# Other orders of the same work on every engine of a two-batch attention and LoRA kernel

## The chip, the cores and the metric

One Trainium2 chip, one core of it. The metric is the device time of one launch in microseconds, the median of several runs. PE is the engine of matrix products and of transposes, PEld its weight loads, DVE the vector engine, ACT the scalar engine, POOL GpSimd, SP the engine that issues most DMAs.

## What is computed

For each of two batches of 1024 tokens (512 features): a layer norm, attention with 32 query heads in 8 groups of 4 (one key and value head per group, rms-normed queries and keys, a causal mask with a slope per head), the output projection, the residual; then a second layer norm and a mixture of 8 LoRA adapters, with its residual.

```python
q = _rmsnorm(q, q_norm_w); k = _rmsnorm(k, k_norm_w)
scores = jnp.einsum('bkgqd,bksd->bkgqs', qg, k) / math.sqrt(HD)
attn = jax.nn.softmax(scores + bias[None], axis=-1)
out = jnp.einsum('bkgqs,bksd->bkgqd', attn, v)
...
x = x + _L0_attn_ref(_layernorm(x, axis=-1), ...)      # out @ Wo.T inside
low = jnp.einsum('bsd,hrd->bshr', x, A)
out = jnp.einsum('bshr,hor,bsh->bso', low, B, scores)
x = x + _L0_ffn_ref(_layernorm(x, axis=-1), ...)
```

## The kernel before

The work is cut into 16 **groups** w = 0 to 15: eight head groups of the first batch, then the same eight of the second. A group holds 8 tiles s of 128 queries, and 4 heads h. The names of the items, as the tables have them:

- `q.8.c` to `q.15.c` and `q.1.c` to `q.7.c`: the projection of one query tile in four parts; `square_q` (ACT), `inv_q` (POOL), `norm_q` (DVE) norm it, `turn.q` transposes it on PE, `high.q` (ACT) and `low.q` (DVE) split it in an upper and a lower fp32r part. A number of 8 or more is a tile of the next group: each group prepares tiles 0 and 1 of its successor, and its keys and values (`turn.kv`, `inv_k`, `norm_k`, `turn.k`, `v_high`, `v_low`).
- `scores.s.h` (PE) into one PSUM tensor of two banks, `max.s.h` (DVE: bias, row maximum, copy to SBUF), `exp.s.h` (ACT), `invert.s.i` (DVE), `normalise.s.h` (POOL).
- The weights of a query tile have to be transposed in tiles j. Some go over PE: `turn.p.s.j`, `high.p`, `low.p`. The others go **through memory**: `send_p.s.h` (SP) stores a head's row to HBM, `fetch_p.s.j` (SP, four DMAs each) loads a tile back in transposed order of blocks, `flip_p.s.j` (DVE) transposes within blocks, `upper_p.s.j` (ACT) and `lower_p.s.j` (POOL) split. The first `fetch_p` of a tile waits until all four sends of it have landed.
- `values.s.j` (PE) accumulates over j, the tiles through memory last, `o_high.s` (ACT) and `o_low.s` (DVE) split the result, `y.s` is the output projection, `add_y.s` (DVE) the residual.
- `x_stats`, `x_moments`, `x_rstd`, `x_norm`, `turn.x`: the first layer norm; `f_...`, `turn.f`, `turn.logits`, `turn.lora`, `f_out`, `add_f`: the second one and the LoRA mixture, one tile at a time.

Every product is done in three matmuls (upper by upper, lower by upper, upper by lower; line 1106). Every transpose on PE goes through one of three PSUM banks in turn.

**What sets the order.** No scheduler runs at build time. Six tables of items stand at the top of the file (lines 27 to 299): `PROLOGUE` (before group 0), `GROUP_A` (groups 0 to 6), `BOUNDARY` (group 7, which also starts the second batch and the first batch's LoRA part), `FIRST_B` (group 8), `GROUP_B` (groups 9 to 14), `LAST` (group 15). `follow` (line 423) goes through them once per engine and emits those items that belong to that engine, so each table is the order of all five engines at once, and each engine executes its items strictly in that order. An item waits for semaphores alone: an item that waits holds up everything behind it on its engine. The semaphores count, so the wait values follow from the positions in the tables.

Tiles through memory and their buffers are set apart from the order: `MEMORY_TILES` says which tiles j of each query tile take that way. In groups 0 to 6 there are two more pairs of split buffers than in group 7; in groups 8 to 15 two more pairs and two more raw buffers (`MORE_SLOTS, MORE_RAW = (2, 0, 2), (0, 0, 2)`).

## Time and profile before

| | us |
|---|---|
| median of 3 runs | 2059.68 |
| lowest, highest | 2056.29, 2061.45 |
| the profiled execution | 2058.6 |
| its span, first to last instruction | 2056.5 |

In that execution PE is busy for 97% of the span, PEld 83%, DVE 66%, POOL 58%, ACT 57%, and the TensorE clock was granted in full for 99.7% of it. In the rows further down a time is microseconds from the start of the span; "[0.74 <-DVE oT_lo L1029]" behind a row is idle time of that engine ahead of it, and what ended it. A PE row's duration overlaps with its successor's, so the distance between two starts says what a matmul takes of the engine, and the idle time in brackets is shorter than the time lost by what the overlap adds.

### The profile page before, as it was taken

To read this page: it belongs to the slowest core of one execution; us is meant where nothing else is said; L and a number is where in the kernel's file an instruction comes from. 1 tells how busy PE (TensorE), PEld (TensorE's weight loads), DVE (VectorE), ACT (ScalarE), POOL (GpSimd) and SP (SyncE) were. 2 spreads that over 40 slices of the span, in tenths; PEclk is the share of its full clock that TensorE was granted. 3 is DMA by queue.
4 is the path that set the end of the run, shared out by engine and by line. 5 is a ranking of instruction groups with operands and counts; after the bars stand their busy time and mean duration, and the time that the engine had idled before them with its cause. 6 is when DMAs were issued, how large, how long until landed. Compare 5 with 4: busy or idle time off the path is not lost.

```text
span 2056.5 us, 33589 instructions
## 1 busy us (share of the span) xinstructions
PE 1993.2 (97%) x10956; PEld 1698.1 (83%) x10956; DVE 1363.5 (66%) x3431; ACT 1162.6 (57%) x3314; POOL 1189.2 (58%) x1188
## 2 busy tenths in 40 slices
PE   7999999999999999999999899999999999999996
PEld 6888888888888888888888788787878878788774
DVE  6667667666666666768876566565666656566696
ACT  4656656565665656655555465555656555465552
POOL 3574645647465574655645557465664746657473
PEclk9999999999999999999999999999999999999998
DMA  4573855657466573765635637365463745637254
GB/s 164 138 161 119 192 141 150 132 154 166 129 171 145 136 159 113 181 181 142 135 109 141 142 96 173 96 154 139 123 124 108 172 101 137 161 81 165 69 122 99
DMA packets 896141, 283.81 MB, mean 138 GB/s; under 512 B 677721, under 2 KB 839513, under 8 KB 895969
## 3 DMA queue, kind: packets, MB, share of 16 engines
q1 hardware_dynamic: 844064, 179.44, 41.7%
q10 hardware_dynamic: 51904, 102.24, 14.2%
q8 instruction: 88, 1.44, 0.3%
q14 instruction: 85, 0.69, 0.1%
HBM read 152.59 MB, written 128.97 MB: 137 GB/s over the span
## 4 chain that ended last, share of the span: by engine, by line
PE 76%; SPq 8%; DMA 4%; DVE 4%; issue 4%; POOL 2%; ACT 2%; DVEq 0%; POOLq 0%; ACTq 0%
PE s_ps L1106 16%; PE q_ps L1106 15%; PE y_ps L1106 14%; PE o_ps L1106 14%; PE turn_ps L1193 9%; SPq L653 7%; PE turn_ps L1106 7%; DMA p_bounce<-probs_odd 2%; POOL probs_odd L881 1%; DMA p_raw_b<-p_bounce 1%; DMA p_bounce<-probs_even 1%; DVE oT_lo L1029 1%; PE turn_ps L1187 1%; SPq L642 1%; ACT oT_hi L823 1%
## 5 line engine op out<-in xcount | busy, mean ns | idle before, releaser
L881 POOL TENSOR_TENSOR probs_odd<-probs_odd,p_inv 128x256 f32<-128x256 f32 (+3 forms) x256 | 318.0, 1257 | 180.1 <-DVE p_inv L1008 179.2
L881 POOL TENSOR_TENSOR probs_even<-probs_even,p_inv 128x128 f32<-128x128 f32 (+3 forms) x256 | 261.3, 1043 | 191.3 <-DVE p_inv L1008 190.5
L1106 PE MATMUL s_ps<-kT_hi,qT_hi 128*128 128x512 f32 (+3 forms) x768 | 272.5, 355 | 4.1 <-DVE neg_max L1001 3.8
L1001 DVE CUSTOM_DVE_ANT_0 probs_odd<-s_ps,rel 128x256 f32<-128x256 f32 (+3 forms) x256 | 209.3, 820 | 97.3 <-issue 96.6
L802 ACT ACTIVATE probs_odd<-probs_odd,neg_max 128x256 f32<-128x256 f32 (+3 forms) x256 | 212.2, 831 | 91.7 <-DVE neg_max L1001 91.6
L1106 PE MATMUL s_ps<-kT_hi,qT_lo 128*128 128x512 f32 (+3 forms) x768 | 262.4, 342 | 0.0
L1106 PE MATMUL s_ps<-kT_lo,qT_hi 128*128 128x512 f32 (+3 forms) x768 | 261.7, 341 | 0.0
L802 ACT ACTIVATE probs_even<-probs_even,neg_max 128x128 f32<-128x128 f32 (+3 forms) x256 | 185.1, 725 | 118.7 <-DVE neg_max L1001 118.4
L1001 DVE CUSTOM_DVE_ANT_0 probs_even<-s_ps,rel 128x128 f32<-128x128 f32 (+3 forms) x256 | 174.9, 687 | 109.8 <-issue 108.8
L987 DVE STREAM_TRANSPOSE p_raw<-p_raw 128x512 f32<-128x512 f32 x252 | 174.9, 700 | 83.5 <-DMA p_raw<-p_bounce 83.2
L1106 PE MATMUL q_ps<-wqT_hi,xnT_hi 128*128 128x512 f32 x512 | 217.2, 424 | 1.0 <-DVE qn L1012 0.8
L1106 PE MATMUL y_ps<-woT_hi,oT_hi 128*128 128x512 f32 x512 | 204.8, 400 | 10.9 <-DVE oT_lo L1029 8.6
L789 ACT ACTIVATE pT_hi<-turn_ps 128x512 fp32r<-128x512 f32 x260 | 154.3, 597 | 107.3 <-PE turn_ps L1193 107.3
L887 POOL TENSOR_TENSOR pT_lo<-p_raw,pT_hi 128x512 fp32r<-128x512 f32 x134 | 173.8, 1301 | 49.7 <-ACT pT_hi L797 49.6
L1106 PE MATMUL q_ps<-wqT_hi,xnT_lo 128*128 128x512 f32 x512 | 201.6, 394 | 0.0
L1106 PE MATMUL y_ps<-woT_hi,oT_lo 128*128 128x512 f32 x512 | 200.5, 392 | 0.0
L1106 PE MATMUL q_ps<-wqT_lo,xnT_hi 128*128 128x512 f32 x512 | 200.4, 391 | 0.0
L1106 PE MATMUL y_ps<-woT_lo,oT_hi 128*128 128x512 f32 x512 | 199.9, 390 | 0.0
L979 DVE TENSOR_TENSOR pT_lo<-turn_ps,pT_hi 128x512 fp32r<-128x512 f32 x260 | 174.8, 677 | 27.2 <-ACT pT_hi L789 26.1
L811 ACT ACTIVATE qn<-q_ps 128x128 f32<-128x128 f32 x512 | 134.7, 280 | 94.9 <-PE q_ps L1106 93.9
L1106 PE MATMUL o_ps<-pT_hi,v_hi 128*128 128x512 f32 x426 | 177.3, 416 | 4.5 <-DVE pT_lo L979 3.7
L1106 PEld LDWEIGHTS s_ps<-kT_hi,qT_hi 128*128 128x128 f32 x768 | 144.6, 188 | 32.0 <-DVE neg_max L1001 9.1
(131 smaller groups left out, 5068.3 us busy)
## 6 DMA issues: line engine op xcount, KB each, us to landing
p_raw<-p_bounce SPq DMA_DIRECT2D x1008, 64.0 KB, 2.3
p_bounce<-probs_odd SPq DMA_DIRECT2D x60, 384.0 KB, 3.1
p_raw_b<-p_bounce SPq DMA_DIRECT2D x256, 64.0 KB, 2.4
p_bounce<-probs_odd SPq DMA_DIRECT2D x60, 256.0 KB, 2.8
p_bounce<-probs_even SPq DMA_DIRECT2D x60, 256.0 KB, 3.0
p_bounce<-probs_even SPq DMA_DIRECT2D x64, 192.0 KB, 2.4
wq_kept<-wqT_hi ACTq DMA_DIRECT2D x8, 1024.0 KB, 4.5
wq_kept<-wqT_lo ACTq DMA_DIRECT2D x8, 1024.0 KB, 6.8
```

Source lines behind the costliest of these rows:

```text
L642: sp.dma_start(p_bounce[s % 2, first:s + 1, h].rearrange("u p c -> p u c"), probs[s % 2][:, h, first * P:(s + 1) * P].rearrange("p (u c) - ...
L653: sp.dma_start(raw_p(n)[b * BLOCK:(b + 1) * BLOCK, :].rearrange("p (n j) -> p n j", j=BLOCK), blocks[b]).then_inc(p_fetched[n], 16)
L789: nc.scalar.activation(target, bank, ACT.Copy).then_inc(sems["high"], 1)
L802: nc.scalar.activation(row, row, ACT.Exp, bias=neg_max[:, s % 2, h:h + 1], scale=-1.0, accum_out=p_sum[:, s % 2, h:h + 1]).then_inc(sems[" ...
L811: last = nc.scalar.activation(qn[:, h, :], q_ps[:, h * HD:(h + 1) * HD], ACT.Square, scale=float(slopes[gg % NG * G + h]), accum_out=q_sum ...
L881: nc.gpsimd.tensor_tensor(row, row, p_inv[:, s % 2, h:h + 1].to_broadcast((P, L)), ALU.mult).then_inc(sems["normalise"], 1)
L887: nc.gpsimd.tensor_tensor(p_low(r), raw_p(raw_tile[w, s, j]), p_high(r).bitcast(F32), ALU.subtract).then_inc(sems["lower_p"], 1)
L979: nc.vector.tensor_tensor(target, bank, upper.bitcast(F32), ALU.subtract).then_inc(sems["low"], 1)
L987: nc.vector.transpose(raw, raw).then_inc(sems["flip_p"], 1)
L1001: nc.vector.tensor_tensor_reduce(out=probs[s % 2][:, h, 0:L], in0=s_ps[:, at_col:at_col + L], in1=rel[:, S - L:S], scale=-float(slopes[w % ...
L1106: last = nc.tensor.matmul(target, a, m, start=start and i == 0 and k == 0, stop=stop and i == len(pairs) - 1 and k == 2)
L1193: last = nc.tensor.transpose(bank[0:width, i * rows:(i + 1) * rows], source, ident[0:rows, 0:rows])
```

## The change

The six tables of items are written in another order. Each table holds exactly the items that it held before (125, 502, 666, 507, 469 and 573), and everything behind them is unchanged but for one line of shift (line 1106 is 1107 afterwards): the same instructions, `MEMORY_TILES`, buffers and rule of waits. No item moves from one table to another. The lines below are the heads of two tables; the rest of the diff is of this kind.

```diff
 PROLOGUE = (
-    "load_y.2 load_y.0 load_y.1 load_y.3 load_y.7 x_stats.2 load_y.4 x_stats.0 load_y.6 x_stats.1 load_wkv.first "
+    "load_y.1 load_y.0 load_y.2 load_y.3 load_wkv.first x_stats.1 x_moments.1 x_stats.0 x_rstd.1 load_wq.first "
...
 GROUP_B = (
-    "back_wkv scores.0.0 scores.0.1 norm_q.1 max.0.0 max.0.1 turn.q.1 exp.0.0 q.2.0 back_wo scores.0.2 high.q.1 q.2.1 "
+    "back_wkv scores.0.0 scores.0.1 norm_q.1 max.0.0 max.0.1 turn.q.1 exp.0.0 q.2.0 high.q.1 q.2.1 exp.0.1 back_wo "
```

**PE, first third of group 0 (table `GROUP_A`), query tile 1.** `s_ps` 128x256 are the scores of tile 1, three matmuls for each head; `w_raw` is a weight being transposed. Before:

```order
L1193 MATMUL turn_ps<-ident,w_raw 128x128 x4
L1106 MATMUL s_ps<-kT_hi,qT_hi 128x256
L1106 MATMUL s_ps<-kT_lo,qT_hi 128x256
L1106 MATMUL s_ps<-kT_hi,qT_lo 128x256
L1106 MATMUL s_ps<-kT_hi,qT_hi 128x256
L1106 MATMUL s_ps<-kT_lo,qT_hi 128x256
L1106 MATMUL s_ps<-kT_hi,qT_lo 128x256
L1106 MATMUL s_ps<-kT_hi,qT_hi 128x256
L1106 MATMUL s_ps<-kT_lo,qT_hi 128x256
L1106 MATMUL s_ps<-kT_hi,qT_lo 128x256
L1193 MATMUL turn_ps<-ident,w_raw 128x128 x4
```

And in the same place now:

```order
L1194 MATMUL turn_ps<-ident,w_raw 128x128 x4
L1107 MATMUL s_ps<-kT_hi,qT_hi 128x256
L1107 MATMUL s_ps<-kT_lo,qT_hi 128x256
L1107 MATMUL s_ps<-kT_hi,qT_lo 128x256
L1107 MATMUL s_ps<-kT_hi,qT_hi 128x256
L1107 MATMUL s_ps<-kT_lo,qT_hi 128x256
L1107 MATMUL s_ps<-kT_hi,qT_lo 128x256
L1194 MATMUL turn_ps<-ident,w_raw 128x128 x4
L1107 MATMUL s_ps<-kT_hi,qT_hi 128x256
L1107 MATMUL s_ps<-kT_lo,qT_hi 128x256
L1107 MATMUL s_ps<-kT_hi,qT_lo 128x256
L1194 MATMUL turn_ps<-ident,w_raw 128x128 x4
```

`turn.wkv.0`, which stood behind head 2, now stands between heads 1 and 2 of tile 1, and `turn.wo.3` (the last row) now stands between heads 2 and 3.

**SP, second half of a group of batch B (table `GROUP_B`).** `p_bounce<-probs_even 128x4x128` are the sends of tile 6, `p_bounce<-probs_odd 128x6x128` those of tile 7 (heads 0 to 3 in order), `x4` of `p_raw` or `p_raw_b` is one `fetch_p`. Before:

```order
L642 DMA p_bounce<-probs_even 128x4x128 x4
L653 DMA p_raw<-p_bounce 32x16x32 x8
L642 DMA p_bounce<-probs_odd 128x6x128
L653 DMA p_raw<-p_bounce 32x16x32 x4
L642 DMA p_bounce<-probs_odd 128x6x128
L653 DMA p_raw_b<-p_bounce 32x16x32 x4
L642 DMA p_bounce<-probs_odd 128x6x128 x2
L653 DMA p_raw_b<-p_bounce 32x16x32 x4
```

And now:

```order
L643 DMA p_bounce<-probs_even 128x4x128 x3
L654 DMA p_raw<-p_bounce 32x16x32 x12
L643 DMA p_bounce<-probs_odd 128x6x128
L654 DMA p_raw_b<-p_bounce 32x16x32 x4
L643 DMA p_bounce<-probs_odd 128x6x128 x3
L654 DMA p_raw_b<-p_bounce 32x16x32 x4
```

`fetch_p.6.5` now stands ahead of `send_p.7.0`, and `fetch_p.6.6` ahead of `send_p.7.1`, so nothing stands between the last three sends of tile 7.

**DVE, group 8 (table `FIRST_B`), from the copy `kv_raw` of the last keys on.** `STREAM_TRANSPOSE` is a `flip_p`, `pT_lo<-turn_ps,pT_hi` a `low.p`. Before:

```order
L952 COPY kv_raw<-turn_ps 128x512
L987 STREAM_TRANSPOSE p_raw<-p_raw 128x512
L979 TENSOR_TENSOR pT_lo<-turn_ps,pT_hi 128x512
L1029 TENSOR_TENSOR oT_lo<-o_ps,oT_hi 128x512
L979 TENSOR_TENSOR pT_lo<-turn_ps,pT_hi 128x512
L987 STREAM_TRANSPOSE p_raw<-p_raw 128x512
L987 STREAM_TRANSPOSE p_raw_b<-p_raw_b 128x512
L1035 TENSOR_TENSOR y<-y_ps,y 128x512
L979 TENSOR_TENSOR pT_lo<-turn_ps,pT_hi 128x512
L1018 TENSOR_TENSOR kv_raw<-kv_raw,k_inv 128x8x128
```

And now:

```order
L953 COPY kv_raw<-turn_ps 128x512 x2
L988 STREAM_TRANSPOSE p_raw<-p_raw 128x512
L1036 TENSOR_TENSOR y<-y_ps,y 128x512
L1030 TENSOR_TENSOR oT_lo<-o_ps,oT_hi 128x512
L980 TENSOR_TENSOR pT_lo<-turn_ps,pT_hi 128x512 x2
L988 STREAM_TRANSPOSE p_raw<-p_raw 128x512
L1019 TENSOR_TENSOR kv_raw<-kv_raw,k_inv 128x8x128
L980 TENSOR_TENSOR pT_lo<-turn_ps,pT_hi 128x512
L988 STREAM_TRANSPOSE p_raw_b<-p_raw_b 128x512 x2
```

The `flip_p.6.6` on `p_raw_b` stood ahead of `add_y.4` and of the last `low.p` of tile 6 (`low.p.6.2`); now it stands behind both.

## Rows read from the trace of the kernel before

**Rows 1.** Busy time by stretch: groups 3, 7, 8, 10 and 15.
```profile
core 0: us, PE busy (x) PEld busy (x) DVE busy (x) ACT busy (x) POOL busy (x), PEclk, DMA share, GB/s
408.70:532.40 123.70, 122.85 (x685) 105.78 (x685) 81.92 (x199) 74.34 (x210) 72.78 (x70) 1.00 0.60 149
903.40:1046.60 143.20, 142.05 (x810) 120.03 (x811) 119.92 (x320) 77.10 (x218) 78.50 (x92) 1.00 0.56 150
1046.60:1176.80 130.20, 124.29 (x675) 105.34 (x675) 83.86 (x218) 69.17 (x205) 74.16 (x74) 1.00 0.57 140
1299.10:1420.50 121.40, 118.69 (x645) 101.41 (x644) 75.45 (x188) 68.89 (x200) 72.97 (x70) 1.00 0.55 131
1908.50:2056.50 148.00, 129.34 (x645) 101.25 (x643) 110.53 (x293) 66.61 (x188) 76.05 (x82) 0.96 0.43 100
```

**Rows 2.** Timeline of PE, group 4: start, duration, engine, line, operation, tiles.
```profile
542.43 0.39 PE L1106 MATMUL s_ps<-kT_hi,qT_hi 128*128 128x256 f32 x1 [0.31 <-DVE neg_max L1001]
542.65 0.28 PE L1106 MATMUL s_ps<-kT_lo,qT_hi 128*128 128x256 f32 x1
542.77 0.28 PE L1106 MATMUL s_ps<-kT_hi,qT_lo 128*128 128x256 f32 x1
...
549.07 0.39 PE L1106 MATMUL q_ps<-wqT_lo,xnT_hi 128*128 128x512 f32 x1
549.30 0.40 PE L1106 MATMUL q_ps<-wqT_hi,xnT_lo 128*128 128x512 f32 x1
```

**Rows 3.** Timeline of PE: `y.7` of group 3, `turn.q.1` of group 10.
```profile
532.37 0.50 PE L1106 MATMUL y_ps<-woT_hi,oT_hi 128*128 128x512 f32 x1 [0.54 <-DVE oT_lo L1029]
...
1303.55 0.63 PE L1193 MATMUL turn_ps<-ident,qn 128*128 128x128 f32 x4 [0.92 <-DVE qn L1012]
```

**Rows 4.** Timeline of PE, end of group 10: `y.6`, `values.7.6`, `values.7.7`.
```profile
1407.84 0.50 PE L1106 MATMUL y_ps<-woT_hi,oT_hi 128*128 128x512 f32 x1 [0.74 <-DVE oT_lo L1029]
...
1416.31 0.50 PE L1106 MATMUL o_ps<-pT_hi_b,v_hi 128*128 128x512 f32 x1 [0.87 <-POOL pT_lo_b L887]
...
1417.88 0.51 PE L1106 MATMUL o_ps<-pT_hi_b,v_hi 128*128 128x512 f32 x1 [0.18 <-POOL pT_lo_b L887]
```

**Rows 5.** Timeline of SP and POOL, group 10, after `scores.7.3` (ended 1388.8).
```profile
1392.90 3.57 SPq L653 DMA_DIRECT2D p_raw_b<-p_bounce  x4
1396.51 1.08 SPq L642 DMA_DIRECT2D p_bounce<-probs_odd  x2
1400.79 1.93 SPq L653 DMA_DIRECT2D p_raw_b<-p_bounce  x4
1409.21 4.15 SPq L653 DMA_DIRECT2D p_raw_b<-p_bounce  x8
...
1391.76 3.75 POOL L881 TENSOR_TENSOR probs_odd<-probs_odd,p_inv 128x1024 f32<-128x1024 f32 x2 [0.61 <-DVE p_inv L1008]
```

**Rows 6.** Timeline of DVE and PE, group 8: `flip_p.6.6`, `low.p.6.2`, `values.6.2`.
```profile
1154.04 0.71 DVE L987 STREAM_TRANSPOSE p_raw_b<-p_raw_b 128x512 f32<-128x512 f32 x1 [3.43 <-DMA p_raw_b<-p_bounce]
...
1155.25 0.67 DVE L979 TENSOR_TENSOR pT_lo<-turn_ps,pT_hi 128x512 fp32r<-128x512 f32 x1
...
1155.98 0.50 PE L1106 MATMUL o_ps<-pT_hi,v_hi 128*128 128x512 f32 x1 [3.03 <-DVE pT_lo L979]
```

**Rows 7.** Timeline of SP, group 8: `fetch_p.6.6` and the last two sends.
```profile
1149.30 2.51 SPq L653 DMA_DIRECT2D p_raw_b<-p_bounce  x4
1151.86 1.08 SPq L642 DMA_DIRECT2D p_bounce<-probs_odd  x2
```

**Rows 8.** Timeline of POOL, group 15: `lower_p.6.3`, the last two norms of tile 7.
```profile
2006.18 1.28 POOL L887 TENSOR_TENSOR pT_lo_b<-p_raw,pT_hi_b 128x512 fp32r<-128x512 f32 x1
2007.64 3.75 POOL L881 TENSOR_TENSOR probs_odd<-probs_odd,p_inv 128x1024 f32<-128x1024 f32 x2 [0.19 <-DVE p_inv L1008]
```

**Rows 9.** Timeline of DVE and PE, the start: first row tile, `q.8.2`.
```profile
3.45 1.33 DVE L907 BATCH_NORM_STATS2 x_stat<-y 128x6 f32<-128x512 f32 x2 [1.63 <-DMA y<-in_L_attn_x]
...
22.54 0.48 PE L1106 MATMUL q_ps<-wqT_hi,xnT_hi 128*128 128x512 f32 x1
```

517 rows, old and new, of tables (BOUNDARY, FIRST_B, GROUP_A, GROUP_B) are left out of this document.

## Prediction

> **What bounds the kernel.** I read the busy times by stretch first [rows 1]. PE is busy for 122.85 of 123.70 us of group 3, 142.05 of 143.20 in group 7, 124.29 of 130.20 in group 8, 118.69 of 121.40 in group 10 and 129.34 of 148.00 in group 15; the next engine is DVE, with at most 119.92 of 143.20. So PE is the bound nearly everywhere, its clock is granted in full, and what an order can win is the time in which PE stands still. How much that is cannot be read from busy time, because successive matmuls overlap in the records. The starts tell it [rows 2]: 0.23 us from one 512-column matmul to the next although each lasts 0.40, and 0.12 for 256 columns. A row's bracket therefore understates a stop: the last matmul's overhang (0.40 - 0.23) and the longer first one behind it (0.50 instead of 0.39 or so) belong to it too. `y.7` of group 3, with 0.54 in its bracket [rows 3], loses about 0.9 against a string without a stop.
>
> Added up over the timeline of PE in this way, the stops are: 10.1 us before the first PE instruction; about 1.5 in each of groups 0 to 6 (2 to 3 in the first two); 3.9 in group 7; 7.9 in group 8; 3.5 to 5 in each of groups 9 to 14; 22.7 in group 15, of which 13 lie in the chain behind the last attention output, whose items stand as before. All of it together is some 83 us, and no more than that can go. PE's own work is the same in either order, so it gives nothing back by itself. What follows goes through the stops and asks of each: how long is the chain that it waits for, how much PE work stands between that chain's start and the waiting item (the **cover**, the sum of the starts' distances of what stands between), and what the new order does to both.
>
> **Batch A, groups 0 to 6.** Two stops have a plain change. `scores.1.2` waits for the row maximum of `scores.1.0` (0.31 in the bracket [rows 2], about 0.6 lost): the chain takes 0.77, the cover was 0.36, one triple of 0.12s. The new order puts `turn.wkv.0`, four transposes, between: cover 0.72, so 0.05 to 0.1 is left and 0.5 won. `y.7` waits for `o_low.7`, a chain of 1.5 behind `values.7.7` with a cover of 0.7 in both orders [rows 3]: stays. The others (0.3, 0.15, 0.15) move here and there. I take -0.6 a group, seven times: -4, bounds 0 and -5 (a new stop as large as the old; and half of what is there gone).
>
> **Group 7.** Its 3.9 us are spread over DVE waits of 0.2 to 0.9; about half of them get a longer cover, while several covers of the tiles through memory shrink by 1 to 4 us, which their slack bears as far as the trace tells. -1.5, bounds 0 and -3.
>
> **Batch B, groups 9 to 14**, is the largest term. Here the stops stand at the end [rows 4]: `y.6` (0.74 in the bracket), `values.7.6` (0.87, for POOL's `lower_p.7.6`) and `values.7.7` (0.18), about 2.7 with the overlap, and they come from one chain. `scores.7.3` ends at 1388.8. POOL norms heads 2 and 3 of tile 7 from 1391.76 to 1395.51, so the last head could be sent from 1395.5 at the latest. It isn't: SP is inside `fetch_p.6.6`, four issues that take 3.57 us from 1392.90, and the two last sends go out from 1396.51 to 1397.59 [rows 5]. They land, `fetch_p.7.2` starts at 1400.79, and six fetches of about 2.1 us each follow until 1413.36; then flip, upper and lower part of the last tile: 29.1 us from `scores.7.3` to the ready `lower_p.7.7`, for a cover of 25.9. In the new order `fetch_p.6.5` and `fetch_p.6.6` stand ahead of the sends of tile 7 and were issued by the time at which POOL ends. The last send then starts with POOL's end, 1.0 to 1.4 earlier (1396.51 - 1395.5, and the wait for the first of the two falls away), and everything behind it moves by the same, since SP runs through from there. The cover is 26.2. So the end stops lose up to 1.4 + 0.3, which is all of their 1.7, and `y.6` is the next in turn. It waits for `o_low.6`; that item now stands behind `flip_p.7.3` on DVE, whose data land some 1.4 earlier too, so I expect it ready at about the time at which PE gets there, and its 1.0 to stay between 0.3 and 1.3. `turn.q.1` (0.92 in the bracket [rows 3]) has the same neighbours and stays. I keep the 0.3 back for it: -1.4 a group, six times: **-8.4**. Bounds: 0 (the fetches are limited by landing and not by SP's place) and -12 (both stops gone, 2.0 a group).
>
> **Group 8.** The same tail: `fetch_p.6.6` takes SP from 1149.30 to 1151.81 and the last two sends follow at 1151.86 [rows 7], while POOL had normed the last head by 1148.85; behind the move, 1.3 earlier. The largest single stop is another: `flip_p.6.6` waits 3.43 for its landing at the head of DVE's queue, and the `low.p.6.2` behind it, which needs no data from memory, holds `values.6.2` (3.03 in the bracket) [rows 6]. The new order puts the flip behind both `low.p`. But PE doesn't win these 3.4: the chain from `scores.7.3` to the last tiles takes 32.2 for a cover of 27.5 in both orders, so most of what is saved early is waited for at `values.7.x`. What is won in the end is what the chain itself becomes shorter, 1.3, the stop at `scores.0.2` (0.8, its cover grows from 0.34 to 2.06) and about 0.9 of small ones: -3, bounds -1 and -6 (the whole 3.4 stays won).
>
> **Group 15.** POOL does `lower_p.6.3` (1.28) ahead of the norms of tile 7, which run from 2007.64 to 2011.39 [rows 8]. The new order norms first, and `exp.7.3` isn't behind the upper part of tile 6 any longer: 2.0 less from `scores.7.3` to the last send. `scores.7.3` itself stands 1.3 of PE work later, and some 2.2 of stops ahead of it get cover. -2.0 + 1.3 - 2.2 = **-2.9**, bounds +2 (the later scores count in full and the rest stays) and -6.
>
> **The start.** PE starts at 10.1 on `turn.x`. The first row tile lands at 3.4 [rows 9] and one follows each 0.6 to 1.8 behind it. The new order loads tile 1 first and norms it first, which makes its `turn.x.1` ready about 3.5 earlier. That is no gain by itself: DVE has 16.5 us of work between 3.4 and 23.2, and `q.8.2` at 22.54 [rows 9] needs the end of it in either order. 0, bounds -1 and +1.5.
>
> **Waits not seen before.** With 2,842 items in other places some covers shrink whose wait the trace doesn't show: in group 7 as above, at `values.7.4` of group 8, at `values.3.0` in batch A. Each has a margin in the trace of before, but the margins are 1 us and less for the worst of them. I take +2, bounds 0 and +8 (0.5 a group, what the small stops of batch A cost now).
>
> **Sum.** -4 - 1.5 - 8.4 - 3 - 2.9 + 0 + 2 = -17.8. The profiled execution took 2058.6, so 2040.8; the median of the runs is 1.1 above it, so **2042**. The bounds of the terms taken together in opposite directions are not likely at once; half of them either way gives about 2033 to 2052.
>
> **Rivals.**
>
> *Nearly every stop goes* (0.12). A search over whole tables may have found cover for `turn.q.1`, `y.6` and `y.7` that I don't credit. For it: DVE has 38% of its time free in group 10 [rows 1]. Against it: `turn.q.1` and `y.7` have the same neighbours. 4 us for batch A, 3 for group 7, 3 x 6 for groups 9 to 14 (their 3.5 to 5 without `turn.q.1`), 4 and 3 for groups 8 and 15, +2 for new waits: -30 in place of -17.8, so 2030 after the same 1.1.
>
> *The order isn't what holds the ends of batch B* (0.14). The stops at `values.7.6` and `values.7.7` recur in each of its groups at the same place, and the fetches into `p_raw_b` come one by one: if `fetch_p.7.2` may not start before the sends have landed and each later one before its raw buffer is free, an earlier send shifts only the first. Against it stands that SP shows its issues without a gap from 1400.79 on [rows 5]. Terms of batch B and group 8's tail are then 0: -4 - 1.5 - 1.7 + 2 = -5, 2054, no change that a measurement tells.
> The Trainium skill ("Perfetto Trace Analysis", Identifying Performance Opportunities) says that the same gap repeating on the engine that should be saturated can mean too little SBUF or PSUM for the next tile. By that rule, nothing is won here without more buffers, and the time is the one just given; the rows of SP speak for its order instead.
>
> *POOL is late for tile 7* (0.06), the case on the other side. In the new order of batch B the four `lower_p.5.2` to `5.5`, 1.28 each [rows 8], stand ahead of the norms of tile 7, where two stood behind the first of them. If `invert.7.0` is ready before POOL has done them, the norms run up to 2 x 1.3 = 2.6 later, the send of the last head too, and 2.6 - 1.4 - 0.3 = +0.9 a group replaces -1.4. It decides where POOL reaches `normalise.7.0` later than `invert.7.0` by over 1.7; in the trace of before POOL still waited 0.61 for the last `invert` [rows 5], which speaks against it. With +5.4 for groups 9 to 14, the same in 7, 8 and 15 (+7.5 instead of -7.4), +2 at the start and the gain of batch A eaten: about +14, 2073.
>
> **Chances.** The forecast has 0.68. 0.3%, 6 us, is about what a measurement of this kernel can tell from no change, so faster means below 2053.5. Faster has the forecast and the first rival, 0.80; same has the second, 0.14; slower the third, 0.06. The range reaches to 2031, near the large gain, and to 2056, which takes in the case of no change and leaves out the slow one.
>
> **What would show it.** In the profile after: the last two sends of tile 7 in groups 9 to 14 right behind POOL's second norm, with no `fetch_p` of tile 6 between, and `fetch_p.7.2` about 11 us after the end of `scores.7.3` instead of 12; the stop at `values.7.6` under 0.3, the one at `y.6` still there; groups 9 to 14 at 120 us instead of 121.4. `scores.1.2` of batch A without a bracket. Group 8: no 3 us bracket at `values.6.2`, but larger ones at `values.7.x`. `q.8.2` within 1 us of 22.5. It would be wrong if SP waits ahead of `fetch_p.7.2` for landings that don't move with the send, if DVE waits at a flip with a `low.p` or `o_low` behind it, or if POOL's norms of tile 7 start later than 3 us after `scores.7.3`.

## Result and profile after

The changed kernel takes 2065.83 us (median of 15 runs, 2062.13 to 2074.69), the kernel before 2058.18 in the same comparison: ratio 1.0045, with a 95% interval of 1.0034 to 1.0055. Forecast were 2042 and a faster kernel; it is slower by 0.45%, 9 us (7.7 between the two medians). Its profiled execution has a span of 2065.3 us against 2056.5.

Busy time by stretch of the changed kernel, the same columns as in [rows 1], groups 3, 7, 8, 10 and 15. Here a stretch goes from the start of one group's first scores to that of the next; the stretches of [rows 1] begin 2.8 to 3.7 us ahead of the first scores, so lengths are compared in the table further down, where both kernels are cut alike:

```profile
core 0: us, PE busy (x) PEld busy (x) DVE busy (x) ACT busy (x) POOL busy (x), PEclk, DMA share, GB/s
414.22:538.79 124.57, 122.83 (x688) 105.99 (x686) 82.09 (x199) 74.24 (x210) 73.91 (x70) 1.00 0.60 148
912.69:1055.50 142.81, 141.44 (x811) 119.77 (x809) 122.11 (x319) 77.70 (x224) 80.03 (x94) 1.00 0.53 140
1055.50:1182.12 126.62, 124.33 (x675) 105.05 (x675) 82.53 (x216) 69.41 (x203) 74.81 (x74) 1.00 0.59 147
1304.50:1425.40 120.90, 118.67 (x645) 101.37 (x644) 75.37 (x188) 69.02 (x199) 73.67 (x71) 1.00 0.55 131
1916.24:2065.30 149.06, 127.49 (x633) 101.40 (x631) 109.16 (x291) 65.15 (x179) 74.86 (x81) 0.94 0.43 99
```

PE's busy time in groups 3, 7, 8 and 10 is what it was, to 0.7 us; what differs is the stops. Group by group, from the starts of the first scores in the two profiles (the differences are taken before rounding):

| stretch | before | after | difference | forecast |
|---|---|---|---|---|
| start | 41.2 | 38.1 | -3.1 | 0 |
| groups 0 to 6 | 865.8 | 874.6 | +8.7 | -4 |
| group 7 | 142.4 | 142.8 | +0.4 | -1.5 |
| group 8 | 130.2 | 126.6 | -3.6 | -3 |
| groups 9 to 14 | 731.6 | 734.1 | +2.5 | -8.4 |
| group 15, to the end of `add_f.7` | 142.7 | 146.5 | +3.8 | -2.9 |

The last column leaves out the +2 for waits not seen before. Group 7's first two weight transposes stand behind its first scores now, which moves 0.7 us from the row of groups 0 to 6 to that of group 7.

**Groups 0 to 6.** All seven have one new stop, ahead of `scores.7.2`, of 0.96 to 2.09 us in its bracket. Timeline of DVE, PE, SP and ACT's DMA queue in group 4 of the changed kernel:

```profile
611.23 1.22 DVE L1002 CUSTOM_DVE_ANT_0 probs_odd<-s_ps,rel 128x1024 f32<-128x1024 f32 x1
612.38 1.30 DVE L988 STREAM_TRANSPOSE p_raw<-p_raw 128x512 f32<-128x512 f32 x2
617.00 0.71 DVE L988 STREAM_TRANSPOSE p_raw<-p_raw 128x512 f32<-128x512 f32 x1 [3.32 <-DMA p_raw<-p_bounce]
617.64 1.22 DVE L1002 CUSTOM_DVE_ANT_0 probs_odd<-s_ps,rel 128x1024 f32<-128x1024 f32 x1
...
618.92 0.50 PE L1107 MATMUL s_ps<-kT_hi,qT_hi 128*128 128x512 f32 x1 [1.60 <-DVE neg_max L1002]
...
605.43 6.77 SPq L654 DMA_DIRECT2D p_raw<-p_bounce  x12
612.29 4.55 SPq L643 DMA_DIRECT2D p_bounce<-probs_even  x4
...
609.70 0.43 ACTq L711 DMA_DIRECT2D w_raw<-in_L_attn_Wo  x1
```

The two `CUSTOM_DVE` rows are `max.7.0` and `max.7.1`, the three transposes `flip_p.5.2` to `5.4`. PE had finished `scores.7.1` at 614.45, but `max.7.1` starts at 617.64, because `flip_p.5.4` stands ahead of it and waits 3.32 us for its data; `scores.7.2` needs the PSUM that `max.7.1` reads. The issue of the fetch's last DMA ended at 612.20 and it landed close to 617.0, 4.8 us later. At 609.70, together with the first of the fetch's four DMAs, ACT issued `load_wo`, 1 MB.

**Groups 9 to 14.** The SP order is what was forecast, and it doesn't bring the gain. Timeline of SP in group 10, after `scores.7.3` (ended 1391.2); POOL's last norms; PE's `values.7.6` and `values.7.7` (compare [rows 4, 5]):

```profile
1393.05 0.43 SPq L643 DMA_DIRECT2D p_bounce<-probs_odd  x1
1393.59 2.47 SPq L654 DMA_DIRECT2D p_raw_b<-p_bounce  x4
1396.10 3.00 SPq L643 DMA_DIRECT2D p_bounce<-probs_odd  x3
1402.74 1.91 SPq L654 DMA_DIRECT2D p_raw_b<-p_bounce  x4
...
1394.03 3.75 POOL L882 TENSOR_TENSOR probs_odd<-probs_odd,p_inv 128x1024 f32<-128x1024 f32 x2 [0.86 <-DVE p_inv L1009]
...
1418.00 0.51 PE L1107 MATMUL o_ps<-pT_hi_b,v_hi 128*128 128x512 f32 x1
...
1420.02 0.51 PE L1107 MATMUL o_ps<-pT_hi_b,v_hi 128*128 128x512 f32 x1 [1.05 <-POOL pT_lo_b L888]
```

Three sends go out in one string from 1396.10 to 1399.10, no `fetch_p` between them, and `fetch_p.7.2` starts at 1402.74: 11.5 us after `scores.7.3` instead of 11.9. The stops at `y.6` and, mostly, at `values.7.6` are gone in all six groups; the one at `values.7.7` has grown (brackets of 1.05 to 2.15, where they were 0.18 to 0.83).

**The clock.** The granted clock is half for a short while behind a stop of PE, in group 2 of the changed kernel, and again in groups 11 and 12 and twice in group 15 ahead of the kernel's end. Busy time in stretches of 2 us, in group 2:

```profile
366.00:368.00 2.00, 0.23 (x1) 0.24 (x2) 1.71 (x4) 0.88 (x2) 0.71 (x1) 1.00 1.07 265
368.00:370.00 2.00, 2.00 (x8) 1.58 (x8) 0.60 (x3) 0.99 (x2) 1.30 (x2) 0.79 0.70 113
370.00:372.00 2.00, 2.00 (x6) 1.52 (x6) 2.00 (x4) 1.17 (x2) 2.00 (x2) 0.50 0.72 113
372.00:374.00 2.00, 2.00 (x9) 1.66 (x8) 0.02 (x1) 1.20 (x6) 2.00 (x2) 0.85 0.77 123
```

In the first 2 us PE worked for 0.23; then the granted clock is 0.79, 0.50 (1.2 of 2.4 GHz) and 0.85 of full speed, and the matmuls of `y.4` lie 1.6 us further apart in sum. Of the seven it is the only group in which this happened; it takes 126.90 where the others take 124.3 to 125.0. The length of the stop alone doesn't tell it: group 2's has 1.92 in its bracket, group 6's 2.09, and there the clock stayed full. One stretch of group 6 and one of group 11, each just behind the stop:

```profile
868.00:870.00 2.00, 1.35 (x6) 1.13 (x7) 0.69 (x3) 1.34 (x3) 1.29 (x1) 1.00 0.99 188
1544.00:1546.00 2.00, 2.00 (x7) 1.51 (x7) 0.69 (x1) 1.55 (x2) 0.00 (x0) 0.50 0.00 0
```

In groups 11 and 12 the half clock comes behind `values.7.7`, and from its start to the next group's first scores PE takes 6.96 us instead of the 5.38 of the groups beside them. These two times 1.6 us are more than the whole +2.5 in the row of groups 9 to 14.

### The profile page after: what moved, and what is told of

Read it like the earlier page. It is cut to its first block, busy times and chain, and to the rows that moved or that the text cites. A ratio compares the mean times of both kernels' runs of the same rounds, so it can differ in the third digit from the quotient of the medians.

```text
span 2065.3 us, 33588 instructions
## 1 busy us (share of the span) xinstructions
PE 1997.0 (97%) x10956; PEld 1704.7 (83%) x10956; DVE 1369.8 (66%) x3431; ACT 1162.0 (56%) x3314; POOL 1197.7 (58%) x1188
## 4 chain that ended last, share of the span: by engine, by line
PE 67%; DMA 8%; DVE 7%; issue 6%; SPq 6%; POOL 3%; ACT 2%; ACTq 0%; POOLq 0%; DVEq 0%
PE q_ps L1107 14%; PE s_ps L1107 13%; PE y_ps L1107 13%; PE o_ps L1107 12%; PE turn_ps L1194 8%; PE turn_ps L1107 6%; SPq L654 6%; DMA p_bounce<-probs_odd 4%; DMA p_raw<-p_bounce 3%; POOL probs_odd L882 2%; DVE p_raw L988 1%; DVE pT_lo L980 1%; DMA p_raw_b<-p_bounce 1%; DVE oT_lo L1030 1%; ACT probs_odd L803 1%
## 5 line engine op out<-in xcount | busy, mean ns | idle before, releaser
L1107 PE MATMUL s_ps<-kT_hi,qT_hi 128*128 128x512 f32 (+3 forms) x768 | 271.3, 353 | 13.3 <-DVE neg_max L1002 11.9
```

Source lines behind the costliest of these rows:

```text
L1107: last = nc.tensor.matmul(target, a, m, start=start and i == 0 and k == 0, stop=stop and i == len(pairs) - 1 and k == 2)
```

## Experiments

A group of lines under an edit is the order of the table, reduced to the items that matter. The ratios are to the kernel before, five rounds each, with their 95% intervals.

### One table at a time

```diff
-GROUP_A = (table of the kernel before)
+GROUP_A = (table of the changed kernel)
```

> The kernel before with the new GROUP_A alone (groups 0 to 6). In the profile of the changed kernel PE stops 1.3 to 2.2 us ahead of scores.7.2 in each of these groups, where it didn't before. Theory Q (the queue of DVE): flip_p.5.4 now stands ahead of max.7.1, its data land 3.3 us after DVE gets to it, and scores.7.2 waits for max.7.1. The loss belongs to this table alone: groups 0 to 6 together 8 to 10 us longer than before, scores.7.2 with a stop of 1.3 to 2.2 in each, time 0.4 to 0.5% above before (about 2067). Theory C (the clock): the granted clock of the whole execution fell from 0.997 to 0.993, which is 8 us of 2060; then this kernel without the new last group shows a clock of 0.996 or 0.997 and at most 2 us. Theory N (the neighbours): the stop comes from where the new table of the start leaves the DMA queues; then it is not there.

1.0037 (1.0024 to 1.0051), 2064.83 us. Groups 0 to 6 take 872.2 us, 6.3 more than before; `scores.7.2` has its stop in each (brackets of 0.81 to 2.18). Theory Q holds, though 6.3 is less than the 8 to 10 expected, and N falls: the stop needs nothing from the other tables. C isn't what carries it: in this profile the clock is full from the first to the last of these groups, and the loss is there.

```diff
-GROUP_B = (table of the kernel before)
+GROUP_B = (table of the changed kernel)
```

> The kernel before with the new GROUP_B alone (groups 9 to 14). In the two profiles the last send of tile 7 starts 6.9 us after the end of scores.7.3 instead of 7.8 (means of six groups), but fetch_p.7.2 only 11.8 instead of 12.0, and lower_p.7.7 ends 29.7 instead of 29.5 behind it. Theory D (the send lands no earlier): groups 9 to 14 are between 1 us shorter and 4 us longer in sum, the time within 0.2% of before. Theory V (chance): the 0.9 us of the earlier send are real and this one profile hid them; then the six groups are 5 us shorter, fetch_p.7.2 at 11.2 or less in the mean, -0.25%.

1.0002 (0.9993 to 1.0011). The send is early again (6.9), `fetch_p.7.2` at 11.8, groups 9 to 14 take 729.3. In the eight profiles taken in this study with the old table these six groups took 726.8 to 733.5, 729.4 in the mean; in the four with the new one 729.3 to 734.1, 732.0. So single profiles differ by more than the two tables do, and the +2.5 of the first comparison is no loss that can be told from none; this profile, the one of the four without a half clock in these groups, has 729.3. The gain forecast, 8.4, is not there: theory D. The same twelve profiles say it of the chain: with the old table the last send starts 7.5 us after `scores.7.3` in the mean and `fetch_p.7.2` at 11.6, with the new one 7.0 and 11.8. The 12.02 of the kernel before's own profile is at the high end.

```diff
-LAST = (table of the kernel before)
+LAST = (table of the changed kernel)
```

> The kernel before with the new LAST alone (group 15). Two places of DVE's queue in the profile of the changed kernel: max.7.3 starts 3.1 us after the end of scores.7.3, behind f_norm.4, low.p.6.1, f_low.3 and low.lora.2; and add_y.6 stands behind flip_p.7.4, whose data land 2 us after y.6 is ready, which turn.f.6 waits for (a stop of 3.4 on PE). Theory Q: group 15 takes 3.5 to 4.5 us longer than before wherever it stands, with the same two waits; +0.2%. Theory C: it is the half clock of 2 to 3 short stretches between 2010 and 2045; where the clock stays at 1.00 there, the group takes at most 1.5 us longer.

1.0022 (1.0012 to 1.0031). Group 15 takes 149.1; with the new table it took 146.5 to 149.1 in four profiles, with the old one 142.5 to 143.9 in eight. `max.7.3` starts 3.10 after `scores.7.3` and `turn.f.6` stops again (3.14 in its bracket). The loss belongs to the table. How much of it is clock (theory C) isn't separated: in this profile the clock is half for 6.8 us of the group, ahead of the half clock at the kernel's end that every profile shows, and in the kernel before for none.

```diff
-PROLOGUE, FIRST_B = (tables of the kernel before)
+PROLOGUE, FIRST_B = (tables of the changed kernel)
```

> The kernel before with the new PROLOGUE and the new FIRST_B (group 8). In the profile of the changed kernel the first scores stand at 38.1 us instead of 41.2 and group 8 takes 126.6 instead of 130.2. Theory S (both gains are real and add up): 6.7 us less, 0.9967 of before, first scores at 38.1 to 38.6, group 8 at 126.6 to 127.5. Theory G (given back later): what comes earlier at the start is waited for again in group 0, or group 9 is longer by what group 8 saved; then at most 2 us of them stay, 0.999.

0.9962 (0.9950 to 0.9975), 2048.07 us. First scores at 38.04, group 8 126.3, group 0 as before: nothing is given back. Theory S.

The four parts, timed apart, make +7.6, +0.4, +4.5 and -7.8 us, +4.7 in sum, against +9.2 for all of it; each is known to 2 or 3 us, so this sum agrees with the whole without proving it. `BOUNDARY` (group 7) wasn't timed by itself.

### Groups 0 to 6: the flip, the load, or both

The changed kernel with tile 5.4 put back:

```diff
 flip_p.5.3 scores.7.1 upper_p.5.2 exp.7.0
-flip_p.5.4
 ...
 turn.kv.0 max.7.1 upper_p.5.3
-upper_p.5.4
 ...
 exp.7.1
-lower_p.5.4 invert.7.0
+upper_p.5.4 invert.7.0 flip_p.5.4
 ... normalise.7.0
+lower_p.5.4
```

> The changed kernel with one tile through memory put back in GROUP_A: flip_p.5.4 behind invert.7.0 (DVE), upper_p.5.4 behind exp.7.1 (ACT), lower_p.5.4 behind normalise.7.0 (POOL), as in the kernel before. Theory Q: max.7.1 runs when scores.7.1 is there, the stop ahead of scores.7.2 is gone in groups 0 to 6 (under 0.2) and nothing takes its place (values.5.4 comes 8 us later), so the groups take 123.3 each instead of 124.9: 9 to 11 us less than the changed kernel, 2055 to 2057, that is -0.1% against before. Theory L (late landing as such): what is late is fetch_p.5.4; the stop moves to values.5.4 or y.5 and at most 3 us are won. Theory C: at most 2 us.

0.9982 (0.9972 to 0.9991), 2052.45 us, below the 2055 to 2057 expected: the three items were worth 0.63% against the changed kernel, and turned it from slower to faster. The stop at `scores.7.2` is gone and none takes its place; groups 0 to 6 take 861.7, 12.9 less than in the changed kernel, of which the seven stops make some 11.4 and the half clock of group 2 1.6. Theory Q, as far as the place of the flip is one way to remove the loss. The landing isn't earlier by it: the fetch's last DMA still lands 4.6 to 6.5 us behind the end of its issue, only nothing urgent waits for it. Then the flip's new place alone, in the kernel before:

```diff
 turn.kv.0
+flip_p.5.4
 max.7.1 ... invert.7.0 scores.7.2
-flip_p.5.4
```

> The kernel before with one item of one table in another place: flip_p.5.4 on DVE directly ahead of max.7.1 instead of behind invert.7.0. SP's order, and so the time at which its data land, is that of before. In the profile of before flip_p.5.4 ran 2.7 us behind the end of scores.7.1. Theory Q: DVE waits for the landing with max.7.1 behind it, scores.7.2 stops for 0.5 to 2.0 us in each of groups 0 to 6, 4 to 12 us in all (+0.2 to +0.6%). Theory F (the fetch): the changed kernel's flip was late only because its fetches 5.2 to 5.4 went out in one string and later; with the fetches of before the data are there when max.7.1 can start, and it costs under 0.3 a group, under 2 us in all.

1.0006 (0.9996 to 1.0015), and groups 0 to 6 take 865.7, to 0.2 us what they took before: no stop at all. Theory F: with SP's and ACT's order of before, the flip waits for 0.17 us at most, as this timeline of DVE in group 4 of that kernel shows (`flip_p.5.4`, then `max.7.1`):

```profile
612.65 0.71 DVE L987 STREAM_TRANSPOSE p_raw<-p_raw 128x512 f32<-128x512 f32 x1 [0.17 <-DMA p_raw<-p_bounce]
613.29 1.22 DVE L1001 CUSTOM_DVE_ANT_0 probs_odd<-s_ps,rel 128x1024 f32<-128x1024 f32 x1
```

The fetch's last DMA lands 1.7 to 2.1 us behind the end of its issue in all seven groups here. So my first reading was half of the cause. The other half is what makes the landing late, and it stands on a third engine:

```diff
 high.p.5.1 invert.6.1
-load_wo
 ... exp.7.2
+load_wo
```

> The changed kernel with one item of GROUP_A in another place: load_wo (ACT's DMA queue, 1 MB of the next output weights) behind exp.7.2 instead of behind invert.6.1. In the profile of the changed kernel it is issued at 609.70 in group 4, just ahead of the four DMAs of fetch_p.5.4 (issued 610 to 612.2, flipped at 617.0, nearly 5 us later, where 2.4 is the median of such a fetch); in the kernel before it is issued at 600.25, 7.7 us ahead of fetch_p.5.4. And flip_p.5.4 put ahead of max.7.1 by itself cost nothing measurable with the transfers of before. Theory B (the queues of the DMA engines): the stop at scores.7.2 is the flip's place times a late landing, and the load is what makes it late; without it the data are there 1 to 2 us earlier, the stop falls from 1.3 to 2.2 us to under 0.6, 5 to 9 us less than the changed kernel (2057 to 2061). Theory P (late fetches): the fetches of tile 5 are late since they start 4.5 us later behind send_p.5.3, whatever else is loaded; then the stop stays over 1 us, under 3 us won.

0.9986 (0.9977 to 0.9995), 2053.91 us: this single item takes the changed kernel from 1.0045 to 0.9986. Theory B, and more of it than expected. Timeline of SP, DVE and ACT's DMA queue in group 4 with the load moved:

```profile
598.73 6.33 SPq L654 DMA_DIRECT2D p_raw<-p_bounce  x12
605.16 0.98 SPq L643 DMA_DIRECT2D p_bounce<-probs_even  x2
...
605.65 2.00 DVE L988 STREAM_TRANSPOSE p_raw<-p_raw 128x512 f32<-128x512 f32 x3
607.77 1.22 DVE L1002 CUSTOM_DVE_ANT_0 probs_odd<-s_ps,rel 128x1024 f32<-128x1024 f32 x1
...
613.30 0.41 ACTq L711 DMA_DIRECT2D w_raw<-in_L_attn_Wo  x1
```

The twelve fetches end at 605.06 and all three flips run through; the third, `flip_p.5.4`, starts no later than 607.0, within 2.0 us of the end of its fetch's last issue, where it was 4.8. Over the seven groups that DMA landed 1.7 to 3.4 us behind its issue, where it was 4.6 to 6.1. Its place on DVE is the bad one still, and costs nothing. The stop needs both: a flip ahead of an item that PE waits for, and 1 MB on the DMA engines while its data travel.

### Groups 9 to 14: what the last send waits for

The kernel before, with `fetch_p.6.6` moved the other way than in the change:

```diff
 send_p.7.1 y.4 lower_p.5.5
-fetch_p.6.6
 ... send_p.7.2 ... send_p.7.3
+fetch_p.6.6
 ...
-flip_p.6.6 upper_p.6.6
 ... add_y.5
+flip_p.6.6 upper_p.6.6
```

> The kernel before with three items of GROUP_B in other places: fetch_p.6.6 (SP) behind send_p.7.3 instead of between send_p.7.1 and 7.2, and for it flip_p.6.6 and upper_p.6.6 behind add_y.5. The last sends then start when POOL ends, 6.6 us after the end of scores.7.3 in every group, with send_p.7.1 still early (the changed kernel holds 7.1 back to about 4.9, and its three sends in a row keep the DMA engines full until they land). Theory W (what counts is how many bytes stand in the DMA queues behind and before the last send): fetch_p.7.2 at 11.0 or less in the mean instead of 11.3 to 12.0, groups 9 to 14 shorter by 0.5 to 1.2 each, time 0.15 to 0.35% below before. Theory D (the landing doesn't move with the send): fetch_p.7.2 at 11.5 to 12 as before, within 0.1%; slower if values.6.6 has to wait for the later fetch_p.6.6 (then a stop is seen there).

0.9961 (0.9949 to 0.9974), 2047.75 us, a little more than the 0.15 to 0.35% expected; groups 9 to 14 take 721.4 instead of 726.8 to 733.5. Timeline of SP in group 10 of that kernel (`scores.7.3` ended 1389.0) and its `values.7.7`:

```profile
1388.68 0.43 SPq L642 DMA_DIRECT2D p_bounce<-probs_odd  x1
1389.22 2.55 SPq L653 DMA_DIRECT2D p_raw<-p_bounce  x4
1391.82 4.14 SPq L642 DMA_DIRECT2D p_bounce<-probs_odd  x3
1396.06 4.63 SPq L653 DMA_DIRECT2D p_raw_b<-p_bounce  x8
...
1415.82 0.50 PE L1106 MATMUL o_ps<-pT_hi_b,v_hi 128*128 128x512 f32 x1 [0.17 <-POOL pT_lo_b L887]
```

The last two sends go out as soon as POOL has normed their heads, 4.75 and 6.60 us after `scores.7.3`; the second goes out at 1391.82, 2.8 behind the scores instead of 4.9 as in the changed kernel; and `fetch_p.6.6` fills the time in which SP used to wait for the landing. The eight fetch DMAs from 1396.06 on are two tiles without a gap, so `fetch_p.7.2` starts at 1398.67, 9.7 us after the scores; in the mean of the six groups it is 10.3, where 11.0 or less was expected and the old table has 11.2 to 12.2. Theory W, with more won than it gave. Its control, the two DVE and ACT items without the fetch:

```diff
-flip_p.6.6 upper_p.6.6
 ... add_y.5
+flip_p.6.6 upper_p.6.6
```

> The kernel before with flip_p.6.6 and upper_p.6.6 of GROUP_B behind add_y.5, and fetch_p.6.6 where it was: the part of the edit that won 8 us that has nothing to do with the sends. Theory W (the sends' landing): the time is within 0.1% of before, fetch_p.7.2 at 11.2 to 12.0 as before; the 8 us belong to the place of the fetch. Theory H (heads of queues): the flip held up add_y.5, norm_q.8 and low.p.6.2 for the landing of tile 6.6, and its move alone wins 3 us or more.

0.9994 (0.9985 to 1.0003), groups 9 to 14 731.9 (one of them, group 12, took 126.05, with 6.8 us of half clock). Not theory H: the 8 us come with the fetch's place. The fetch moved without the two items wasn't run.

### Group 15: which queue

```diff
 f_norm.4 scores.7.3
+max.7.3
 low.p.6.1 ... f_low.3 low.lora.2 values.5.5
-max.7.3
 ...
+add_y.6 f_stats.6 f_moments.6 f_rstd.6 f_norm.6
 flip_p.7.4 ...
-add_y.6 ... f_stats.6 ... f_moments.6 ... f_rstd.6 ... f_norm.6
```

> The kernel before with the new LAST, in which max.7.3 stands directly behind scores.7.3 (it stood behind f_norm.4, low.p.6.1, f_low.3 and low.lora.2), and add_y.6, f_stats.6, f_moments.6, f_rstd.6 and f_norm.6 ahead of flip_p.7.4 (add_y.6 and the rest stood behind it and flip_p.7.5). Theory Q: max.7.3 starts 0.05 after scores.7.3 instead of 3.1, the last send 2 to 3 us earlier, and the stop of 3.3 us ahead of turn.f.6 falls under 1; group 15 takes 4 to 6 us less than with the new LAST unchanged (149.1 and 146.5 in two profiles), 142 to 144, the time -0.05 to +0.1% against before. Theory U (DVE is full here, so that an item moved ahead only pushes another back): under 1.5 us won.

1.0021 (1.0011 to 1.0032), no better than the new table as it is (1.0022); group 15 takes 145.8 in its profile. `max.7.3` started 0.95 instead of 3.1 after `scores.7.3` (not 0.05: `f_norm.4` is still ahead of it), and the norms ended 1.1 earlier, but `fetch_p.7.2` still came 15.3 us after it; the stop at `turn.f.6` (3.14 in its bracket) became one of 2.07 at `values.7.3` and one of 2.42 at `turn.lora.5`. My two places on DVE were not the cause. The SP rows of the changed kernel show what held the sends:

```profile
2014.76 0.36 SPq L687 DMA_DIRECT2D out<-y  x1
2015.22 1.06 SPq L643 DMA_DIRECT2D p_bounce<-probs_odd  x2
2016.33 1.07 SPq L687 DMA_DIRECT2D out<-y  x1
2017.44 2.08 SPq L643 DMA_DIRECT2D p_bounce<-probs_odd  x2
2023.17 0.86 SPq L654 DMA_DIRECT2D p_raw_b<-p_bounce  x2
```

Heads 0 and 1 of tile 7 were normed at 2008.5 and 2010.6. `store.2` stands ahead of them and waits for `add_f.2` until 2014.76, so all four sends (384 KB each) leave within 4.3 us, and `fetch_p.7.2`, which waits for the last to land, starts 3.6 us behind that. Two items moved:

```diff
-store.2
 ... send_p.7.0 ... send_p.7.1
-store.0
 send_p.7.2 ... send_p.7.3
+store.2 store.0
```

> The kernel before with the new LAST in which two items of SP stand elsewhere: store.2 and store.0 behind send_p.7.3 instead of ahead of send_p.7.0 and send_p.7.2. In the profile of the changed kernel store.2 waits for add_f.2 until 2014.76, so send_p.7.0 and 7.1 go out 4.7 to 6.7 us after POOL had normed them, and fetch_p.7.2 starts 5.8 us after normalise.7.3 ends instead of 4.7. Theory V (volume ahead of the last send, as in groups 9 to 14): with two of the four sends gone early fetch_p.7.2 starts 14.0 to 14.6 us after scores.7.3 instead of 15.4 to 15.6, and group 15 takes 1 us less or a little more than with the new LAST as it is (146.5 to 149.1 in four profiles). Theory N (no part): fetch_p.7.2 stays at 15.4.

1.0005 (0.9995 to 1.0015) where the table as it is has 1.0022; group 15 takes 143.9. Theory V. Timeline of SP, with `scores.7.3` ended at 2005.10:

```profile
2005.94 9.15 SPq L643 DMA_DIRECT2D p_bounce<-probs_odd  x4
2015.13 1.32 SPq L687 DMA_DIRECT2D out<-y  x2
2017.51 1.99 SPq L654 DMA_DIRECT2D p_raw_b<-p_bounce  x4
```

The sends follow the norms over 9 us, and `fetch_p.7.2` comes at 12.4 instead of 15.4, earlier than the 14.0 to 14.6 expected. With DVE's order mended as well:

```diff
+max.7.3 (directly behind scores.7.3), exp.7.3 ahead of o_high.5, invert.7.1 ahead of low.f.4
```

> The same, and max.7.3 directly behind scores.7.3, exp.7.3 ahead of o_high.5, invert.7.1 ahead of low.f.4. If the loss of group 15 is these two queues (DVE's ahead of max.7.3, SP's ahead of send_p.7.0): fetch_p.7.2 at 12.5 to 13.5 us after scores.7.3, which is that of before (13.6) or less, and group 15 at 143 to 144.5, within 0.1% of before. If the rest of DVE's order (f_norm.6, f_gate.5 and the flips in between) costs by itself: still 145 or more, though the fetch is as early as before.

1.0006 (0.9998 to 1.0015), group 15 143.8, though `fetch_p.7.2` starts at 10.3, 3.3 earlier than in the kernel before (whose 13.6 is the latest of the eight profiles with the old table; six of them have about 12.0). From here on the fetch isn't what decides: `flip_p.7.2` still runs 19.0 us after `scores.7.3`, behind other items. The expected interval of the fetch (12.5 to 13.5) was too cautious, that of the group held.

### The parts that won, together

The new PROLOGUE, BOUNDARY and FIRST_B; the new GROUP_A with tile 5.4 put back; GROUP_B of before with the sends first; LAST of before.

```diff
-GROUP_B, LAST = (tables of the changed kernel)
+GROUP_B = (that of the kernel before, fetch_p.6.6 behind send_p.7.3, flip_p.6.6 upper_p.6.6 behind add_y.5)
+LAST = (that of the kernel before)
```

> The parts that won, together: the new PROLOGUE, the new GROUP_A with flip_p.5.4, upper_p.5.4 and lower_p.5.4 put back, the new BOUNDARY and FIRST_B; GROUP_B of before with fetch_p.6.6 behind send_p.7.3 and flip_p.6.6 and upper_p.6.6 behind add_y.5; LAST of before. If the parts add up: 3.1 at the start, 0.6 in each of groups 0 to 6, 3.6 in group 8, 8 in groups 9 to 14 and 1 in group 7, 19 to 20 us, 0.990 to 0.992 of before (2036 to 2040). If they take from one another (what is early in one table is waited for in the next): 0.993 or more.

0.9907 (0.9893 to 0.9920), 2038.04 us. The parts add up: groups 0 to 6 861.1, group 8 127.6, groups 9 to 14 719.8.

```diff
 FIRST_B: -fetch_p.6.6 (ahead of send_p.7.1)   +fetch_p.6.6 (behind send_p.7.3)
 LAST:    invert.7.1 ahead of o_low.5, exp.7.3 ahead of upper_p.6.3, lower_p.6.3 behind normalise.7.3
```

> The best parts together, and two further edits: in the new FIRST_B fetch_p.6.6 behind send_p.7.3, and in LAST of before invert.7.1 ahead of o_low.5, exp.7.3 ahead of upper_p.6.3, and lower_p.6.3 behind normalise.7.3, which is the step of the prediction on group 15 taken by itself (2.0 less from scores.7.3 to the last send). Expected against the best parts alone: group 15 1 to 2 us shorter, with normalise.7.3 ending 7.7 us after scores.7.3 instead of 8.9; group 8 between 0 and 1 us shorter. -0.1%. If DVE's full queue takes it back as it did with the new LAST: group 15 within 0.5 of 142.7.

0.9899 (0.9885 to 0.9912), 2035.94 us, the best of the study: 1.0% below the kernel before, 1.4% below the changed one. Group 8 takes 125.1 and group 15 142.4 in its profile, 2.5 and 1.3 less than in the one above; the two times can't be told apart (their intervals overlap). `normalise.7.3` ends 7.7 after `scores.7.3` as expected, but 142.4 is also within 0.5 of 142.7, the mark set for "taken back", so what the prediction's step on group 15 is worth stays open.

## Why the prediction was wrong

**What bounds the kernel** held: PE's work was the same, and all of the difference is in its stops. So did the sizes of the stops that were read from the trace: in groups 1 to 6 `scores.1.2` started 0.59 us behind the matmul ahead of it and now 0.15, where 0.12 is no stop; `y.7` and `turn.q.1` stayed as they were (0.54 and 0.92 in the bracket). No forecast had the clock: one short half clock in group 2, one each in groups 11 and 12, 1.6 us each.

**Batch A** (-4 forecast, +8.7 in the profile). The step that failed is the one on waits not seen before, "+2, bounds 0 and +8". I compared covers of PE's waits and took the landing of each tile as it had been. But the change also moved the 1 MB load, and put a flip whose margin hung on it ahead of `max.7.1`. The list of what would prove me wrong had "DVE waits at a flip with a `low.p` or `o_low` behind it", but the sum priced no such wait in batch A, and here it was a `max` that stood behind. With the load moved or the flip put back the same table takes 861.7, 4.2 less than before (0.7 of it the two transposes), which is the -4 of the forecast.

**Groups 9 to 14** (-8.4, the largest term; none that can be measured). "Everything behind it moves by the same" failed. The last send did start earlier, 6.95 instead of 7.82 us after `scores.7.3` in the mean of six groups, but `fetch_p.7.2` started at 11.81 instead of 12.02. (Over all twelve profiles it is no earlier at all, 11.8 against 11.6.) It waits for all four sends, and the change bought the last one's early start by holding the second back behind `fetch_p.6.6`: from 3.4 to 4.9 us in group 10, from 3.9 to 5.5 in the mean. What has to land is a volume: with three sends of 384 KB in one string, the fetch starts 3.6 us behind the last issue, where it was 3.2 behind a string of two and 2.7 where the last send went out by itself (the kernel with the sends first); groups 9 and 14, with 4.4 to 5.2 in both kernels, are a case of their own (see the last section). The stop at `y.6`, which the forecast kept, went, and `values.7.7`, the end of the same chain, took it over. The mechanism, SP's order around the last sends, was the right one: done the other way round it gave 8 us, the size forecast. That also settles the second rival. What it said of these groups, no gain, came true for the wrong reason, and in that the 0.14 was luck: the gaps did come from the order. The Trainium skill's rule ("Perfetto Trace Analysis", Identifying Performance Opportunities), that a gap repeating on the busy engine can mean too little SBUF or PSUM, doesn't fit here; the same buffers gave 0.39%.

**Group 15** (-2.9, +3.8). The prediction followed POOL's order to the norms and there stopped. The norms didn't move forward but back (ended 9.6 instead of 8.9 after `scores.7.3`), as `max.7.3` stood behind 3 us of other DVE work; and on SP, `store.2` had come ahead of the first send. The terms ahead of `scores.7.3` (+1.3 and -2.2) aren't the loss: it ended 0.3 later in its group, and 3.5 of the 3.8 us arose behind it. Of a step that is moved each queue that it passes counts, and SP wasn't looked at here. The two stores carry 0.17 of the 0.22%; with them moved, 1.0005 (0.9995 to 1.0015), no loss can be told any more. What the half clock adds in this group stays open.

**Group 8** (-3, -3.6) came out as worked. Its 3 us stop at `values.6.2` is gone; one of 0.57 in the bracket at `values.7.1` is what it left.

**The start** (0, -3.1). "`q.8.2` needs the end of it in either order" was wrong: it starts at 19.44 instead of 22.54 [rows 9]. PE's first item, `turn.x.1`, starts at 6.02 instead of 10.10 (3.5 earlier was forecast), and 3.1 of these 4.1 us stay. DVE's 16.5 us up to 23.2 contain statistics and splits of tiles that `q.8.2` doesn't need; the new order does those behind, and DVE's idle time ahead of 10 us (the brackets of [rows 9]) was time that could be won.

**Group 7** (-1.5, +0.4, or -0.3 without the two transposes): within its bounds.

**POOL late for tile 7**, the case on the slow side, wasn't what happened: `normalise.7.0` did start 2.3 us later, but `normalise.7.3` ended 6.57 us after `scores.7.3` as before. The slower time came from two mechanisms that I had priced in none of the cases, the load beside the flip and the stores ahead of the sends, so 0.06 for slower was far too little for a change over tables of 2,842 items.

## What to carry over

In an order that is written out, an item that waits for a transfer is a wait for everything behind it on its engine, and its margin is set by what else is on the DMA engines, which is a third engine's order; here a load of 1 MB, issued beside a fetch, made its last DMA land 4.6 to 6.1 us behind the issue instead of 1.7 to 3.4, so a margin of 1 to 2 us on a landing isn't safe when large loads move. Before a last send is pulled forward, count the bytes that have to land, not the time of the last issue: spread the sends over the time in which their data come ready, and put fetches that are not urgent behind them, into the wait for the landing. When a whole order is exchanged, time its tables one by one: here the same change held -0.4%, +0.4% and +0.2%.

## What the hardware showed unexpectedly

- A 1 MB load on ACT's queue held up 64 KB fetches on SP's: 4.6 to 6.1 us from the end of the last issue to its landing in the seven groups, against 1.7 to 3.4 with the load moved. DMA queues of two engines share what carries them. The Trainium skill says so too ("DMA: Bandwidth & Descriptors", Queues, rings and completion order: each has one ring on each of the same 16 engines), and this case's rows agree.
- The landing of the last send differs from group to group with the same instructions, and by a pattern: in the changed kernel `fetch_p.7.2` starts 3.6 to 3.7 us behind the end of the last send's issue in groups 10 to 13, and 5.1 and 5.2 in groups 9 and 14 (in the kernel before 3.2, and 4.4 and 4.8). In groups 9 and 14 one packet of a queue that the profile calls "instruction" passes while the last send is under way, in the others none. The DMA queues of the changed kernel in group 9 (1276 to 1281), then in group 10 (1398.5 to 1402), each view's columns being packets, MB and share of 16 engines:

```profile
q1 hardware_dynamic: 2249, 1.11, 78.5%
q8 instruction: 1, 0.02, 1.2%
...
q1 hardware_dynamic: 1989, 1.00, 98.2%
```

Over the 16 profiles there are 96 such landings. In the 28 with this packet at least 0.3 us behind the start of the last send the fetch came 3.6 to 5.3 us behind the issue's end, in the other 68 2.5 to 3.8; where the packet of group 14 had come before the last send (the last two kernels of group 15), group 14 had 3.2. That the packet is the cause is read from the traces, no run tests it.
- The half clock followed one of the seven stops at `scores.7.2`, the one with 1.92 in its bracket, and none of those of 0.96 to 1.60; but neither did it follow the one of 2.09, nor one of 2.18 in the kernel with the new `GROUP_A` alone; in that group it cost 1.6 us, nearly as much again as the stop.
